# Row maxima on ScalarE's queue, the last weights in four groups, and a new planned order

## The reference

```python
# block 0, then block 1 (the same form); gelu MLP 128 -> 512 -> 128
x = x + gate_a * (attention(modulate(ln(x))) @ W_proj + b_proj)          # layer 0 / 2, self
x = x + attention(q=ln(x), kv=ln(context) or context) @ W_cproj + b      # layer 1 / 3, cross
x = x + gate_m * (gelu(modulate(ln(x)) @ W1 + b1) @ W2 + b2)             # layer 7 / 8
# block 2: one cross attention on modulated ln(x) and modulated ln(context)  (layer 4)
# block 3: attention in shifted windows of 64 tokens (layer 5), then
scores = einsum('bqhd,bkhd->bhqk', q, k) / sqrt(8)
top_s, top_i = top_k(scores, 16)                                          # layer 6: 16 of 256 keys
o = softmax(top_s) @ v[top_i]
x = x + g_mlp * (silu(a) * b @ w_m2 + b_m2)                               # layer 9, swiglu
```

## Time and profile before

| | us |
|---|---|
| median of three runs (705.32 to 709.05) | 707.75 |
| the profiled execution's own time | 701.35 |
| its span, first to last instruction | 699.6 |
| TensorE busy in it | 604.1 (86%) |
| VectorE busy | 492.8 (70%) |
| ScalarE busy | 397.3 (57%) |
| GpSimd busy | 243.9 (35%) |

### The profile page before, as it was taken

The page is one execution under the profiler, slowest core; times in us unless marked ns, Lnnn a source line. Parts: engine busy times, 40 slices in busy tenths (PEclk is TensorE's granted clock), DMA queues, the critical chain, the costliest instruction groups (busy, mean ns, idle before and its releaser), DMA issues.

```text
span 699.6 us, 14550 instructions
## 1 busy us (share of the span) xinstructions
PE 604.1 (86%) x5168; PEld 406.2 (58%) x5168; DVE 492.8 (70%) x1307; ACT 397.3 (57%) x677; POOL 243.9 (35%) x471
## 2 busy tenths in 40 slices
PE   4779999999997898999988899987998597878778
PEld 3555655656564456566555555665666365656456
DVE  2665876586256827773547697989989899999921
ACT  3437687888775577789845446534576144423212
POOL 7820532643632123244416013634216215332201
PEclk9859999999898799999979556997599559977698
DMA  8840322220045022202234300222002200300000
GB/s 317 213 169 2 62 63 63 63 62 2 9 86 123 31 62 62 63 2 62 45 80 115 70 2 2 55 68 62 2 11 61 61 2 2 69 2 4 6 1 8
DMA packets 21797, 39.24 MB, mean 56 GB/s; under 512 B 2592, under 2 KB 6752, under 8 KB 21344
## 3 DMA queue, kind: packets, MB, share of 16 engines
q1 hardware_dynamic: 21008, 37.83, 22.0%
q10 hardware_dynamic: 720, 0.49, 0.2%
HBM read 7.96 MB, written 0.52 MB: 12 GB/s over the span
## 4 chain that ended last, share of the span: by engine, by line
PE 39%; DVE 28%; ACT 11%; issue 7%; DMA 6%; POOL 5%; SPq 4%; ACTq 0%; POOLq 0%
PE psum L1198 9%; PE psum L1174 6%; DVE maxima L1013 6%; ACT softmax_T L903 5%; DVE left L1026 5%; PE psum L1144 5%; DVE left L1036 4%; DVE top L1023 4%; DVE top L1033 4%; SPq L727 4%; PE psum L1080 3%; PE psum L1233 3%; DMA qk_stack<-centred 3%; DMA qk_stack<-qk_parts 3%; PE psum L1244 2%
## 5 line engine op out<-in xcount | busy, mean ns | idle before, releaser
L903 ACT ACTIVATE softmax_T<-psum 128x1024 f32<-128x1024 f32 (+1 forms) x224 | 210.7, 965 | 128.9 <-PE psum L1174 65.9
L1013 DVE TENSOR_REDUCE maxima<-psum 128x4 f32<-128x1024 f32 x160 | 189.3, 1216 | 51.5 <-PE psum L1144 51.0
L1198 PE MATMUL psum<-softmax_T,values 128*32 128x256 f32 (+1 forms) x1792 | 133.7, 419 | 8.4 <-ACT softmax_T L903 6.7
L1174 PE MATMUL psum<-qk_stack 32*128 32x256 f32 (+1 forms) x896 | 115.2, 360 | 22.9 <-DMA qk_stack<-centred 11.7
L1174 PEld LDWEIGHTS psum<-qk_stack 32*128 32x128 f32 x896 | 74.9, 218 | 69.2 <-issue 27.9
L1144 PE MATMUL psum<-qk_stack 32*128 32x256 f32 (+1 forms) x768 | 94.8, 362 | 18.5 <-DMA qk_stack<-qk_parts 5.9
L832 POOL TENSOR_SCALAR unpicked<-left 128x512 bf16<-128x512 f32 x64 | 39.7, 621 | 163.3 <-DVE left L1036 162.0
L1144 PEld LDWEIGHTS psum<-qk_stack 32*128 32x128 f32 x768 | 62.9, 222 | 51.2 <-issue 25.0
L1198 PEld LDWEIGHTS psum<-softmax_T,values 128*32 128x32 f32 x1792 | 58.7, 121 | 45.2 <-ACT softmax_T L903 12.4
L792 POOL TENSOR_TENSOR qk_parts<-qk_parts 128x256 fp32r<-128x256 f32 x56 | 40.8, 729 | 66.1 <-ACT qk_parts L886 65.6
L773 POOL TENSOR_SCALAR neg_mean<-mean_var 128x2 f32<-128x2 f32 x48 | 9.2, 193 | 137.5 <-DVE mean_var L1001 137.0
(11 more groups left out here) (98 smaller groups left out, 866.2 us busy)
## 6 DMA issues: line engine op xcount, KB each, us to landing
qk_stack<-qk_parts SPq DMA_DIRECT2D x112, 256.0 KB, 4.7
weights<-in_w SPq DMA_DIRECT2D x1, 2368.0 KB, 11.9
weights<-in_w SPq DMA_DIRECT2D x1, 1408.0 KB, 13.3
row_biases<-in_rows SPq DMA_DIRECT2D x1, 1088.0 KB, 10.4
weights<-in_w SPq DMA_DIRECT2D x1, 832.0 KB, 9.0
qk_stack<-centred SPq DMA_DIRECT2D x48, 8.0 KB
x<-in_x SPq DMA_DIRECT2D x1, 512.0 KB, 4.6
context<-in_ctx SPq DMA_DIRECT2D x1, 512.0 KB, 7.4
```

The costliest lines, as they stand in the source:

```text
L903: nc.scalar.activation(pT[:, slot, u % 2, :, 0:cols].rearrange("p (i t) n -> p i t n", t=NT), two_banks(step).rearrange("p i (t n) -> p i ...
L1013: nc.vector.tensor_reduce(rows[:, u // 4, u // 2 % 2, g:g + 2, :], ps.rearrange("p i (t k) -> p i t k", t=NT), AX_X, ALU.max).then_inc(fin, 1)
L1174: ins = nc.tensor.matmul(ps[:, i, t, 0:P if window else N], QKS[b][32 * g:32 * g + 32, s, 1, P * t:P * t + P], QKS[b][32 * g:32 * g + 32, ...
L1198: ins = nc.tensor.matmul(misc[32 * g:32 * g + 32, queries], V[:, b, t, first:first + 32], pT[:, slot, g // 2, 2 * (g % 2) + t, 0:P if wind ...
```

## The change

1. The step that ScalarE does for row maxima now waits for its own copy and then issues the transfer itself, on ScalarE's queue. SyncE has 64 steps fewer. The copy for the second group of heads still waits until the first transfer has landed.
2. `WGROUPS` has eight groups. The last four (8, 9, 8 and 12 blocks) are steps of SyncE's planned list (`load`).
3. The statistics of the context are taken once for each batch. GpSimd makes the second centred context from them, after the first one has been transposed.
4. `plan` follows the transfer queue: a stack takes 1.25 us of it and a block of weights 0.195, one after the other. ScalarE's maxima step costs 0.95 instead of 0.26. A planned wait of 0.3 (before: 0.5) gets spare matmuls, for 0.95 (before: 0.75) of it. `LEAD` and `BIAS` have new numbers, and a table `EXTRA` adds one for each engine, kind, batch and place in the chain.

```diff
-           WAT["L2_xcond_Wss_q"], NW]
+           WAT["L2_xcond_Wss_q"], WAT["L3_xcond_w_ada"], WAT["L3_xcond_w_qkv"], WAT["L3_xcond_w_m1"], NW]
+
+LATER = {4: 38.0, 5: 70.0, 6: 85.0, 7: 100.0}
...
-    ("pe", "maxima"): 0.33, ("act", "maxima"): 0.26, ("sp", "maxima"): 0.65,
+    ("pe", "maxima"): 0.33, ("act", "maxima"): 0.95,
...
-IDLE, SPARE_SHARE, SPARE_D, SPARE_CELLS = 0.5, 0.75, 0.24, 0.2133
+IDLE, SPARE_SHARE, SPARE_D, SPARE_CELLS = 0.3, 0.95, 0.24, 0.2133
...
-LANDS = 2.0
-STACK_LANDS = 4.0
+
+TO_QUEUE, STACK_TIME, LANDS, AHEAD = 1.9, 1.25, 0.6, 1.75
...
+EXTRA = {
+    ("act", "context", 0, 0): 4.6, ("act", "context", 0, 1): 24.0, ("act", "context", 0, 2): -2.2,
...
-        return tail[t] + lead[b][CHAIN.index(l % CTX_NORM)] + BIAS.get((eng, kind), 0.0)
+        return tail[t] + lead[b][CHAIN.index(l % CTX_NORM)] + BIAS.get((eng, kind), 0.0) + EXTRA.get(
+            (eng, kind, b, CHAIN.index(l % CTX_NORM)), 0.0)
...
+        if eng == "sp" and kind == "stack":
+            moves = max(end + TO_QUEUE, queue)
+            free[eng] = end = max(end, moves - AHEAD)
+            queue = moves + STACK_TIME
+            land = queue + LANDS
...
-LEAD = [[35.7, 32.6, 90.2, 32.5, 34.5, 183.3, 33.4, 51.2, 73.3, -13.5],
...
+LEAD = [[22.6, 23.7, 18.9, 23.7, 23.1, 31.1, 24.3, 23.5, 66.9, -397.7],
...
-                    stacks_sent += 1
-                    if stacks_sent == 8:
-                        load_w(last_group)
-                elif kind == "maxima":
-                    after(sp, "act", step)
...
+                elif kind == "load":
+                    load_w(l)
...
-                    after(pool, "dve", ("stats", b, l, 0))
+                    if l == CTX_NORM + 4:
+                        after(pool, "pe", ("normed", b, CTX_NORM + 1, 0))
+                    else:
+                        after(pool, "dve", ("stats", b, l, 0))
...
                     nc.scalar.activation(z[0:rows, b, :, :], misc[0:rows, 0:N].rearrange("p (t f) -> p t f", t=NT),
                                          ACT.Copy).then_inc(fin, 1)
+                    act.wait_ge(fin, NTH["act", step])
+                    if ATTN[l]["kind"] == "topk":
+                        act.dma_start(QKS[b][31::32, u, 0, :].bitcast(F32),
+                                      z[0:4, b, :, :].rearrange("p t f -> p (t f)")).then_inc(max_in[b], 16)
+                    else:
+                        act.dma_start(QKS[b][31::32, 2 * u:2 * u + 2, 0, :].bitcast(F32),
+                                      z[0:NH // 2, b, :, :].rearrange("p t f -> p (t f)")).then_inc(max_in[b], 16)
```

More of the change, by code:

```diff
@@ new lines @@
+BIAS = {
+    ("act", "context"): 101.8, ("act", "heads_out"): -0.8, ("act", "k_parts"): 34.3, ("act", "maxima"): 4.0,
+    ("act", "mix"): 93.7, ("act", "normed"): 9.4, ("act", "qk"): -1.2, ("act", "up"): 0.8, ("act", "values"): 9.0,
+    ("act", "weights"): 2.7, ("dve", "divide"): 73.6, ("dve", "down"): -42.4, ("dve", "gates"): 10.3,
+    ("dve", "mods"): 46.3, ("dve", "pbias"): -3.2, ("dve", "residual"): 82.1, ("dve", "scores"): -13.4,
+    ("dve", "stats"): 10.7, ("dve", "topk"): 247.8, ("dve", "topk_rest"): 79.7, ("dve", "up_gate"): -233.8,
[3 rows of a table added]
+    ("pool", "gated"): -7.1, ("pool", "k_parts"): 47.3, ("pool", "pre"): -6.2, ("pool", "qk"): -1.5,
+    ("pool", "topk"): 62.7, ("pool", "z"): -11.4, ("sp", "load"): -261.8, ("sp", "stack"): 24.4,
+    ("sp", "store"): 6.0,
@@ L264, in plan @@
         step = ("pbias", 0, l, 0)
-        pbias_of[l] = task("dve", step, task("pe", step))
+        pbias_of[l] = task("dve", step, task("pe", step, *[loads.get(w_group(ATTN[a]["o"])) for a in range(first, last)]))
     for b in range(B):
@@ L362, in busy @@
             d = 1.4
-        if kind == "mix" and ATTN[l]["kind"] == "window":
+        if kind == "mix" and ATTN[l]["kind"] == "window" and eng == "pe":
             d = 0.6
@@ L377, in plan @@
     for t in reversed(_sorted(order, deps)):
-        tail[t] = busy(t) + (lands.get(t[1][0], 0.0) if t[0] == "sp" else 0.0) + max(
+        tail[t] = busy(t) + (transfer(t[1]) if t[1][0] == "load" else lands.get(t[1][0], 0.0) if t[0] == "sp" else 0.0) + max(
             (tail[n] + HOP for n in users[t]), default=0.0)
@@ L398, in plan @@
     clock, spare = Clock(), {}
-    table, last = "exp", 0
+    table, last, queue = "exp", 0, 16.0
     def takes(t):
@@ L510, in plan @@
             had[ring, step] = sorted({before for _, _, before in which if before is not None})
-        land = end + lag + (lands.get(kind, 0.0) if eng == "sp" else 0.0)
+        land = end + lag
+        if eng == "sp" and kind == "stack":
[3 more added lines that the diff above has]
+            land = queue + LANDS
+        elif eng == "sp" and kind == "load":
+            moves = max(end + TO_QUEUE, queue)
+            free[eng] = end = max(end, moves - AHEAD)
+            queue = moves + transfer(step)
+            land = queue + LANDS
+        elif eng == "act" and kind == "maxima":
+            land = end + TO_QUEUE + 0.3
         for r, taker in gives(t):
-            slots[r] += [(land + HOP, k, taker) for k in slot[r, taker]]
+            slots[r] += [((end if kind == "maxima" else land) + HOP, k, taker) for k in slot[r, taker]]
             slots[r].sort()
```

265 lines of the change are left out of this document (225 added, 40 removed), and 179 rows, old and new, of tables (BIAS, EXTRA, LEAD).

## The result

Before: 706.54 us median of 4 runs (702.24 to 709.05). Changed: 686.76 us median of 4 (678.3 to 697.16), ratio 0.9625, 95% interval 0.9534 to 0.9715. The profiled execution of the changed kernel took 680.88 us, 679.0 of it span. The ratios leave out executions more than 1.5% above a kernel's fastest, among them the profiled ones of q6 (736.7 us), q10 (717.1) and q11 (705.7); where executions spread as widely as here (678 to 697 us), a difference by ratios and one by medians are some us apart, and I give both.

The account below looks back on a forecast made before the run. Bound by TensorE's work before the first top-k head, VectorE's from there to the last, then a serial tail: 430 + 231 + 30 = 691 us of span, 692.8 with the 1.75 around it, x 1.009 = 699 us; range 680 to 724.

Parts of the forecast that it names:

- much faster rival: Whole kernel: TensorE packs at full clock before the first head, floors elsewhere; 670 us of span, 678 scaled; chance 0.18.
- VectorE block: First to last top-k head: 225 us of VectorE work plus 6 of waits, 231 us instead of 267.
- without gaps over 3 us: Sign: VectorE has no gap over 3 us from the first to the last head, some 231 us.
- I take 0, bound 23: Spare matmuls in the VectorE part: no cost taken; the largest block (32) could cost up to 23 us of TensorE.
- The start: Up to the first weights matmul: split weights and earlier maxima bring it to 37.3 from 45.2 us; 6 us taken.
- The first head: End of the TensorE part: first top-k head at 430 us, from a bound of 424 to 432; sign 422 to 438.
- less 5% for the clock: TensorE from 76 us to the first head: 352 us of work, less 5%, at 0.939 busy makes 356 us.
- slower rival: Before the first head: TensorE packs no better; first head 460 us, 731 scaled; turning point 439 us; chance 0.29.
- hidden, up to 8 us lost: ScalarE before the first head: 47 maxima issues (28 us) hidden on average at 0.81 busy, up to 8 us lost.
- The tail: After the last top-k head: 32.2 us, less 4.4 for spares, plus 2 for batches meeting, gives 30; ceiling 38.
- 4.4 us lost, and they are gone: Tail: eleven spare matmuls ran to 689 us while centred was ready at 684.6; removing them saves 4.4 us.
- third rival: Start and maxima waits: engines still serve bulk first, 45.2 us start stays; 700 us of span, 708 scaled; chance 0.15.

Follow-up runs that it names:

- q6: Changed kernel with a second, unread 64-byte transfer issued by ScalarE behind each of the 64 maxima transfers; 727.0 us, ratio 1.0286.
- q10: Changed kernel with GpSimd issuing the maxima transfers and without the spare matmuls ahead of batch 1's layer 6 maxima and weights; 717.6 us, ratio 1.0092.
- q11: Kernel before, in its old order, with GpSimd instead of SyncE issuing the maxima transfers; 700.7 us, ratio 0.9936.
- q2: Changed kernel's order and statistics, with maxima back on SyncE's queue and the last weights in one transfer behind the eighth stack; 705.0 us, ratio 1.000.
- q5: Changed kernel, maxima still issued by ScalarE, but SyncE also waits for each maxima copy at q3's places; 693.9 us, ratio 0.9825.
- q8: Changed kernel without the spare matmuls ahead of batch 1's layer 6 maxima (32) and weights (13); 679.9 us, ratio 0.9612.
- q12: Kernel before without the eleven spare matmuls ahead of batch 1's last layer; 704.8 us, ratio 1.0011.
- q1: Kernel before, in its old order, with only the maxima transfers moved to ScalarE's queue; 712.8 us, ratio 1.008.
- q4: Changed kernel with the last 37 blocks of weights in one transfer behind the eighth stack, maxima on ScalarE's queue; 688.8 us, ratio 0.974.
- q3: Changed kernel with only the maxima transfers back on SyncE's queue, the first behind the sixteenth stack, four weights groups kept; 702.0 us, ratio 0.9963.
- q7: Changed kernel without any of its spare matmuls; 684.9 us, ratio 0.9658.

## Why the prediction was right, and where it was not

The forecast was 699 us, the result 686.8: on the expected side and inside the range, but below the forecast's own 693 to 706, and a little nearer to the much faster rival (678) than to the forecast. The sum held because the parts were priced together. Split into order and queue it would have failed, as q2 shows, and that the total came out on the right side is in part luck. By the prediction's own steps:

**VectorE block: right.** 231 predicted, 232.6 measured, 233 to 234 in q2 to q5 whatever the queues do. Its make-up was off, and two errors cancel: I took 6 us of waits and there were 13.8 for picks alone, so everything else took about 218 where I counted 225 (in q8 too: 223.7 less 5.7). One wait of 6.9 us also breaks my sign "without gaps over 3 us". The spares were priced "I take 0, bound 23"; they cost 7 to 9 us there.

**The start: right in the sum, and not by the queue's landing time.** First weights matmul foreseen at 37.3, measured 37.06. The copy ended at 32.7 (I had 33.8) and the transfer took 4.2 (I had 3.5). The prediction called the 6.00 us of the old profile the price of standing behind bulk on one queue. The runs don't bear that out: on that queue, behind that bulk, the transfer took 3.48 us in q12 and 3.76 in q2 (issued 1.5 and 1.8 us later), on ScalarE's queue 3.39 in q1 and 5.15 in q4; in the changed kernel the first of the last weights is issued only at 40.63, after the transfer has landed. The prediction set two sentences of the Trainium skill against each other: that another issuer saves issue time only (DMA: Bandwidth & Descriptors, "Issuing engines are not separate DMA queues"), and that an engine takes packets from its rings in turn (same page, "Queues, rings and completion order"). No run here decides between them.

**The first head: 430 predicted, 420.1 measured,** below the 422 to 438 of my signs. The step that was mis-sized is the TensorE work with "less 5% for the clock": 352 us were to become 334. From 76 us on it was 292.6 + 24.4 = 317 us, at a packing of 0.92 of 344 us rather than 0.939. Some 7 of the 17 us are work that had moved ahead of 76 us (434 records from 26 to 76 us where there were 362; 72 at 0.097 us each, an estimate from the table), which the forecast had in its start of 68 to 76 us. The rest is mostly the clock, which was better than taken: 0.98 in the long window, and 0.95 in the join instead of the 0.72 of the earlier trace rows.

**The queue: wrong in kind.** I gave the order nearly all of the gain and the queue 6 us at the start and half of 4.8 us of waits. Without the queue the first head is at 443.6, beyond the 439 that I had named as the turning point of the slower rival; less the 8.8 us of the first transfer's place it would be 435, an estimate, so on which side the order alone falls is open. The gains in block (which that rival had too) and tail only pay for the late head (ratio 1.000 in q2). I had read a late transfer as TensorE's wait for it. In the profiles of the new order what is late costs twice: as idle (9.0 us more in q3 than in the changed kernel) and as clock (14.9 us more busy time for the same records, at 0.90 instead of 0.96).

**ScalarE's issues: "hidden, up to 8 us lost": wrong.** ScalarE at 0.81 busy looked like cover. A second issue of 0.66 us each cost 40 to 47 us. What the first issue costs in the new order can't be read off, because nothing I ran issues them for free. If they cost at least their length, as the added ones did, it is 47 x 0.545 = 26 us, an estimate.

**The tail: 30 predicted, 26.3 measured.** The saving "4.4 us lost, and they are gone" holds for the start of the last layer, and not for its length; in the old kernel it gives nothing (q12). Instead TensorE is at clock 1.00 through the new tail (0.89 in the earlier trace rows), with two batches ending together and a few spares between them; without spares (q7) the same tail runs at 0.79 and takes 29.6 us. Up takes 3.45 us and down 3.58, and the 2 us that I added for the batches' meeting did not come.

**Own queue no help, and statistics once.** The third rival fell: the start did not keep its 45.2 us, and q3 shows that the queue helps in this order. The statistics were not tried by themselves; they are part of every run in the new order.

**Open.** What SyncE's maxima cost if the first is issued where its copy is done. Whether SyncE's waiting (q5) costs time, and why its profile shows it as a lower clock and not as idle time. How much of q4's and q5's longer busy time belongs to their edits and how much to the execution that was profiled.

## What to carry to other kernels

Two edits that do nothing alone can be worth 3 to 4% together: here the tighter order needed the short path between engines, and the short path was worth nothing while the order left other waits behind it. When you put one half back to test the other, look where the steps that you move end up: one transfer held back for 7 us can make up a good part of what you then measure. Before you cost an edit on an engine that is "81% busy" at nothing, double the edit and time it. Compare busy time for the same number of records beside idle time: where TensorE is the bound, stalls can come back as a lower clock.

## What the runs showed of the hardware

An issue of a small transfer took ScalarE 0.545 us (median of 48), SyncE 0.583 and GpSimd 0.627. The first 8 KB of maxima landed in 3.48, 3.76 and 6.00 us behind bulk on SyncE's queue (q12, q2, old kernel) and in 3.39 and 5.15 us from ScalarE's queue beside bulk (q1, q4). After 9 us in which TensorE worked 2.6 (q12), its granted clock was 0.64 for the next 8, and sixteen matmuls that took 3.69 us took 5.84. In the block of q7 the granted clock was 0.59; VectorE's waits for picks were 6.0 us there and 5.7 in q8 at 0.75, its other waits 4.4 and 0.2.
